# Cross-attention values in 32-column tiles of TensorE: the value blocks of two heads stationary, the probabilities moving, the softmax sums by selector matmuls

## What is computed

```python
q = (x @ Wq + bq).reshape(bs, n_ctx, HEADS, d)            # 16 batches x 256 tokens, 16 heads, d = 16
kv = (data @ Wkv + bkv).reshape(bs, n_data, HEADS, 2 * d) # 77 context rows
scores = jnp.einsum('bqhd,bkhd->bhqk', q, k) * scale
attn = jax.nn.softmax(scores, axis=-1)
out = jnp.einsum('bhqk,bkhd->bqhd', attn, v).reshape(bs, n_ctx, WIDTH)
return out @ Wp + bp
# then x = x + that; layer norms; router logits, top 2 of 8 experts, gates, gated expert FFN
```

## Time and profile before

| | us |
|---|---|
| median of 3 runs | 933.84 |
| lowest, highest | 932.91, 934.47 |
| the profiled execution | 936.83 |
| its span in the trace | 935.0 |
| attention rounds, about | 32 to 312 |

### The profile page before, as it was taken

One profiled execution on the slowest core, in us unless ns is written; L12 is line 12 of the kernel. 1 busy time (PEld: TensorE's weight loads), 2 busy tenths in 40 slices (PEclk: granted clock), 3 DMA queues, 4 the chain that ended last, 5 costly groups with the idle time before them and its releaser, 6 DMA issues.

```text
span 935.0 us, 19225 instructions
## 1 busy us (share of the span) xinstructions
PE 891.6 (95%) x6206; PEld 800.3 (86%) x6206; DVE 747.5 (80%) x1757; ACT 647.7 (69%) x1305; POOL 412.6 (44%) x649
## 2 busy tenths in 40 slices
PE   4999999999999999999999999999999999999994
PEld 3787888888878887888999999898898998998994
DVE  2677888888888889787979888887877877778883
ACT  3666767677676774776968777766876777677773
POOL 3455577777777667340432230505214234052042
PEclk9899999999999999999999999999999999999998
DMA  5332242343246337643755454826817737465442
GB/s 141 61 69 50 53 106 67 75 108 74 61 116 192 114 106 281 183 116 116 221 142 172 130 166 151 243 91 186 302 25 230 265 77 261 166 179 178 146 80 26
DMA packets 132626, 129.18 MB, mean 138 GB/s; under 512 B 59985, under 2 KB 117409, under 8 KB 132385
## 3 DMA queue, kind: packets, MB, share of 16 engines
q1 hardware_dynamic: 119648, 110.36, 38.2%
q0 software_dynamic: 12864, 17.44, 10.1%
HBM read 102.01 MB, written 25.36 MB: 136 GB/s over the span
## 4 chain that ended last, share of the span: by engine, by line
PE 79%; DVE 7%; ACT 5%; issue 4%; POOL 2%; SPq 1%; DMA 1%; ACTq 0%; DVEq 0%; POOLq 0%
PE bank L2002 35%; PE bank L2046 18%; PE bank L1835 7%; PE bank L1755 3%; PE bank L1994 3%; PE bank L1812 3%; PE bank L1773 2%; PE bank L2034 2%; PE bank L1971 1%; PE bank L1820 1%; DVE maxes L1256 1%; PE bank L1868 1%; PE bank L1858 1%; ACT q_t L943 1%; PE bank L1802 1%
## 5 line engine op out<-in xcount | busy, mean ns | idle before, releaser
L859 POOL DMA_INDIRECT out_rows<-yo,token x68 | 114.3, 1682 | 380.5 <-ACT yo L1111 314.7
L2002 PE MATMUL bank<-xh,wh 128*128 128x512 f32 (+1 forms) x672 | 234.2, 349 | 3.7 <-DVE gate_in L1628 3.1
L2002 PE MATMUL bank<-xl,wh 128*128 128x512 f32 (+1 forms) x672 | 228.4, 340 | 0.0
L2002 PE MATMUL bank<-xh,wl 128*128 128x512 f32 (+1 forms) x672 | 228.0, 339 | 0.0
L1604 DVE TENSOR_TENSOR wl<-raw,wh 128x1024 fp32r<-128x1024 f32 x126 | 152.4, 1220 | 12.9 <-ACT wh L1042 12.0
L2002 PEld LDWEIGHTS bank<-xh,wh 128*128 128x128 f32 x672 | 127.9, 190 | 17.9 <-DVE gate_in L1628 6.0
L2046 PE MATMUL bank<-wh,hh 128*128 128x256 f32 x496 | 142.1, 286 | 0.5 <-DVE yo L1663 0.3
L2046 PE MATMUL bank<-wh,hl 128*128 128x256 f32 x496 | 140.8, 284 | 0.0
L2046 PE MATMUL bank<-wl,hh 128*128 128x256 f32 x496 | 140.8, 284 | 0.0
L2002 PEld LDWEIGHTS bank<-xh,wl 128*128 128x128 f32 x672 | 127.5, 190 | 14.8
L2002 PEld LDWEIGHTS bank<-xl,wh 128*128 128x128 f32 x672 | 128.0, 190 | 10.7
(11 more groups left out here) (198 smaller groups left out, 1887.4 us busy)
## 6 DMA issues: line engine op xcount, KB each, us to landing
raw<-in_W SPq DMA_DIRECT2D x42, 1024.0 KB, 6.5
raw<-in_Wo SPq DMA_DIRECT2D x25, 1024.0 KB, 5.9
whole<-in_W SPq DMA_DIRECT2D x8, 1024.0 KB, 8.3
xs<-in_x SPq DMA_DIRECT2D x32, 128.0 KB, 2.6
out_rows<-x SPq DMA_DIRECT2D x32, 128.0 KB, 1.8
shared<-z_rows SPq DMA_DIRECT2D x7, 520.0 KB, 5.3
bo_row<-in_bo SPq DMA_DIRECT2D x25, 128.0 KB, 4.4
k_blocks<-k_parts SPq DMA_DIRECT2D x128, 19.2 KB
```

Source lines behind the costliest of these rows:

```text
L859: e.indirect_dma_start(out=out, out_offset=bass.IndirectOffsetOnAxis(ap=token[j % 4][:, s:s + 1], axis=0), in_=yo[j % 2][:, s, :], in_offs ...
L2002: mm = e.matmul(ps[:, h * cols:(h + 1) * cols], ws[split_before(j) % 2][:, w, c, m * P:(m + 1) * P], xx[j % 2][:, c, 0:cols], start=(h == ...
```

## The change

The values product is turned round. The probabilities' columns are now cut into five blocks for each half of eight heads (four of 128 keys, one of 104), ten in all as before, and `probs_t` is the moving operand, 128 tokens wide. The stationary operand is a piece of `v_blocks` of 32 columns, two heads. Its output goes to 32 of the 128 partitions (a quadrant `q`), so each matmul uses 32 columns of the array. Per half there are two passes `s` over the four quadrants, because the 154 keys of two heads lie in two neighbouring blocks: 16 matmuls. The result has the attention columns on the partitions and the tokens along the row, the form that `project` needs.

The column of ones is gone. `sum_probs` multiplies each block of `probs_t` with a constant 32-column selector, again in a quadrant (block number modulo 4), and leaves four partial sums per head. `sums_copy` on ScalarE takes values and sums out of PSUM together. One round later, right behind `scores(i, 0)`, `transpose_sums` adds the four quadrants and turns the sums with one matmul; VectorE takes the reciprocal (`invert_sums`), ScalarE repeats each one 16 times (`widen_inverses`), TensorE turns these (`spread_inverses`, the last step before `scores(i, 1)`) and VectorE multiplies (`normalize`, ahead of the second half of its softmax work), writing `attn_t`. `transpose_attn` and `attn_t_copy` are gone, and "spread" takes the place of "attn" among the bank turns, at another place. `sum_probs` waits for all three copies of the probabilities at once.

Around it: `load_values` issues four DMAs instead of two, `spread_values` four operations instead of six, a table `select` (128 x 336) is loaded at the start, VectorE clears the rows of `v_rep` that no load writes before `setup_ready`, and two small copies of `probs_t` become one.

```diff
@@ misc_turns
-        uses = [("attn", i - 2)] if 0 <= i - 2 < NT else []
-        uses += [("k", nb // 2)] if batch and even and nb % 2 == 0 else []
+        uses = [("k", nb // 2)] if batch and even and nb % 2 == 0 else []
         uses += [("v", nb)] if batch and even else []
         uses += [("q", nb)] if batch and not even else []
+        uses += [("spread", i - 2)] if 0 <= i - 2 < NT else []
         uses += [("logits", i - 5)] if 0 <= i - 5 < NT else []
@@ ScalarE
+            def sums_copy(i):
+                e.wait_ge(values_mm, i + 1)
+                if i:
+                    e.wait_ge(sums_t_mm, i)
+                    e.wait_ge(attn_made, i)
+                e.activation(sums[:, :], value_bank[:, 0:(DC + 1) * P], ACTF.Copy).then_inc(
+                    sums_out, 1)
+
+            def widen_inverses(i):
+                e.wait_ge(recip_made, i + 1)
+                if i:
+                    e.wait_ge(spread_mm, i)
+                e.activation(inverses[:, :].rearrange("p (h d) -> p h d", h=HEADS),
+                             recip[:, :].unsqueeze(2).broadcast_to([P, HEADS, HD]),
+                             ACTF.Copy).then_inc(inverses_out, 1)
...
-                    attn_t_copy(i - 2)
+                    widen_inverses(i - 2)
...
                     exp_scores(i, 1)
+                if before:
+                    sums_copy(i - 1)
@@ VectorE
+            def invert_sums(i):
+                e.wait_ge(sums_t_mm, i + 1)
+                if i:
+                    e.wait_ge(inverses_out, i)
+                at = (DC + 1) * P
+                e.reciprocal(recip[:, :], value_bank[:, at:at + HEADS]).then_inc(
                     recip_made, 1)
+            def normalize(i):
+                e.wait_ge(sums_out, i + 1)
+                e.wait_ge(spread_mm, i + 1)
+                if i >= 2:
+                    e.wait_ge(proj_mm, i - 1)
+                e.tensor_tensor(attn_t[i % 2][:, :, :].rearrange("p c k -> p (c k)"),
+                                sums[:, 0:DC * P], misc_of("spread", i)[:, 0:DC * P],
                                 ALU.mult).then_inc(attn_made, 1)
...
                     softmax_input(i, 0)
+                if 0 <= i - 2 < NT:
+                    invert_sums(i - 2)
...
+                if 0 <= i - 2 < NT:
+                    normalize(i - 2)
                 if 0 <= i < NT:
                     softmax_input(i, 1)
...
-                if 0 <= i - 1 < NT:
-                    normalized(i - 1)
@@ TensorE
+            def transpose_sums(i):
+                at = (DC + 1) * P
+                e.wait_ge(sums_out, i + 1)
+                if i:
+                    e.wait_ge(recip_made, i)
+                e.matmul(value_bank[:, at:at + HEADS], sums[:, DC * P:(DC + 1) * P], select[:, S_PICK:S_END],
+                         start=True, stop=True, skip_group_check=True).then_inc(sums_t_mm, 1)
+
+            def spread_inverses(i):
+                ps = claim("spread", i)
+                e.wait_ge(inverses_out, i + 1)
+                for m in range(DC):
+                    mm = e.transpose(ps[:, m * P:(m + 1) * P],
+                                     inverses[:, m * P:(m + 1) * P], ident)
+                mm.then_inc(spread_mm, 1)
...
+            def sum_probs(i):
...
+                e.wait_ge(probs_t_out, 3 * i + 3)
+                for k in range(KB):
+                    q, size = k % QUADS, P if k < KB - DC else TAIL
+                    mm = e.matmul(
+                        value_bank[q * QUAD:(q + 1) * QUAD, DC * P:(DC + 1) * P],
+                        select[0:size, S_SUM + k * QUAD:S_SUM + (k + 1) * QUAD],
+                        probs_t[i % 2][0:size, k, :], start=(k < QUADS),
+                        stop=(k + QUADS >= KB), skip_group_check=True)
+
             def values(i):
                 b = i // 2
-                if i:
-                    e.wait_ge(attn_made, i)
                 if i % 2 == 0:
-                    e.wait_ge(v_spread, 6 * (b + 1))
-                for k in range(KB):
-                    if k % 4 == 0:
-                        e.wait_ge(probs_t_out, 3 * i + k // 4 + 1)
-                    first, nh = block_heads(k)
-                    size = P if k < KB - 1 else TAIL
-                    mm = e.matmul(
-                        value_bank[:, first * VW:(first + nh) * VW], probs_t[i % 2][0:size, k, :],
-                        v_blocks[b % 2][0:size, k, 0:nh, :].rearrange("p j d -> p (j d)"),
-                        start=(k == 0), stop=(k == KB - 1), skip_group_check=True)
+                    e.wait_ge(v_spread, 4 * (b + 1))
+                for m in range(DC):
+                    for s in range(2):
+                        for q in range(QUADS):
+                            k, size = block_at(m, q + s), block_rows(q + s)
+                            mm = e.matmul(
+                                value_bank[q * QUAD:(q + 1) * QUAD, m * P:(m + 1) * P],
+                                v_blocks[b % 2][0:size, m, s, q, :, :].rearrange(
+                                    "p h d -> p (h d)"),
+                                probs_t[i % 2][0:size, k, :], start=(s == 0), stop=(s == 1),
+                                skip_group_check=True)
                 mm.then_inc(values_mm, 1)
...
                     scores(i, 0)
+                if 0 <= i - 2 < NT:
+                    transpose_sums(i - 2)
...
-                if 0 <= i - 2 < NT:
-                    transpose_attn(i - 2)
...
                     queries(nb)
+                if 0 <= i - 2 < NT:
+                    spread_inverses(i - 2)
...
                 if 0 <= i - 1 < NT:
+                    sum_probs(i - 1)
                     values(i - 1)
```

More of the change, by code:

```diff
@@ L34 @@
 KEYS = HEADS * CTX
-KB = -(-KEYS // P)
-TAIL = KEYS - (KB - 1) * P
-BLOCK_HEADS = 3
-VW = HD + 1
+HALF_KEYS = HPC * CTX
+JB = -(-HALF_KEYS // P)
+KB = DC * JB
+TAIL = HALF_KEYS - (JB - 1) * P
+QUAD = 32
+QH = QUAD // HD
+QUADS = P // QUAD
 WIDTH = 512
@@ L178, with block_at, block_rows, sum_selectors @@
 X_END = X_E + 1
-def block_heads(i):
-    first = i * P // CTX
-    last = min(i * P + P - 1, KEYS - 1) // CTX
-    return first, last - first + 1
+S_SUM = 0
+S_PICK = KB * QUAD
+S_END = S_PICK + HEADS
+def block_at(m, j):
+    return m * (JB - 1) + j if j < JB - 1 else DC * (JB - 1) + m
+def block_rows(j):
+    return P if j < JB - 1 else TAIL
+def sum_selectors():
+    c = np.zeros((P, S_END), np.float32)
+    p = np.arange(P)
+    for m in range(DC):
+        for j in range(JB):
+            at = S_SUM + block_at(m, j) * QUAD
+            key = j * P + p[0:block_rows(j)]
+            c[p[0:block_rows(j)], at + m * HPC + key // CTX] = 1.0
+    for q in range(QUADS):
+        c[q * QUAD + np.arange(HEADS), S_PICK + np.arange(HEADS)] = 1.0
+    return c
 def constants():
@@ L194, in constants @@
     c[:, C_IOTA:C_IOTA + P] = p[None, :]
-    for i in range(KB):
-        first, n = block_heads(i)
-        for j in range(BLOCK_HEADS):
-            c[:, C_VMASK + i * BLOCK_HEADS + j] = (i * P + p) // CTX == first + j
+    for s in range(2):
+        for q in range(QUADS):
+            for h in range(QH):
+                c[:, C_VMASK + (s * QUADS + q) * QH + h] = (
+                    ((q + s) * P + p) // CTX == q * QH + h)
     c[:, C_TOKEN:C_TOKEN + NT] = p[:, None] + P * np.arange(NT)[None, :]
@@ L382, in build @@
         q_l = [sb(f"q_l{i}", [P, DC, SEQ], F32R) for i in range(2)]
-        v_blocks = [sb(f"v_blocks{i}", [P, KB, BLOCK_HEADS, VW]) for i in range(2)]
+        v_blocks = [sb(f"v_blocks{i}", [P, DC, 2, QUADS, QH, HD]) for i in range(2)]
         probs = [sb(f"probs{i}", [P, HEADS, CTX]) for i in range(2)]
@@ L393, in build @@
         xs = [sb(f"xs{i}", [P, D]) for i in range(XR)]
-        attn = [sb(f"attn{i}", [P, D]) for i in range(2)]
+        select = sb("select", [P, S_END])
+        sums = sb("sums", [P, (DC + 1) * P])
         attn_t = [sb(f"attn_t{i}", [P, DC, P]) for i in range(2)]
-        recip = [sb(f"recip{i}", [P, HEADS]) for i in range(2)]
+        recip = sb("recip", [P, HEADS])
+        inverses = sb("inverses", [P, D])
         x1 = [sb(f"x1_{i}", [P, D]) for i in range(3)]
@@ L441, in build @@
         misc, (last_on_bank6, last_on_bank7) = misc_turns()
-        misc_read = {"ctx": lambda b: (ctx_t_out, b + 1), "attn": lambda i: (attn_t_out, i + 1),
+        misc_read = {"ctx": lambda b: (ctx_t_out, b + 1), "spread": lambda i: (attn_made, i + 1),
                      "q": lambda b: (q_out, 2 * b + 2), "proj": lambda i: (x1_made, i + 1),
@@ L816, in pool_program @@
             e.memset(zeros[:, :], 0.0).then_inc(zeros_ready, 1)
-            for i in range(2):
-                e.memset(v_sb[i][:, :, HD:VW], 1.0).then_inc(ones_ready, 1)
             e.memset(mv[:, :, :, :], 1.0).then_inc(mv_ready, 1)
@@ L1165, in drain_rest @@
                     logits_copy(i - 5)
+                if i - 1 < NT:
+                    sums_copy(i - 1)
+                if i - 5 < NT:
```

(11 more changed lines are left out.)

107 lines of the change are left out of this document (47 added, 60 removed).

## The result

The changed kernel takes 958.33 us (median of 4 runs, 955.48 to 961.61), beside it the kernel before 934.15 us (4 runs, 932.91 to 935.64). The ratio is 1.026, with a 95% interval of 1.022 to 1.030: slower by 24 us, where 43 were forecast. The profiled execution spans 956.4 us, against 935.0. So the sign was right and the sum was 19 us too high, and the trace shows that this was not one size a little off. The largest term had the wrong sign, and the loss lies where the sum put next to nothing.

The account below looks back on a forecast made before the run. The prediction took TensorE's queue as the bound. Its terms summed to +1.34 us a tile, times 32 = 43 us, plus 0.3, giving a forecast of 977 us; the range was 928 to 1005.

Parts of the forecast that it names:

- The values block: TensorE's selector and value matmuls: 52 instructions take 2.94 us against 2.15 before, +0.79 us a tile.
- four at a time: Rival for the values matmuls: all four quarters stream side by side, block 1.5 us, total time 931 us; chance 0.16.
- two-at-a-time case: Likeliest case for the values matmuls: two instructions stream together, block 2.94 us, total time 961 to 1003 us; chance 0.62.
- Change of tile shape: TensorE entering and leaving the 32-column tiles around the values matmuls: +0.1 us a tile (0 to 0.2).
- Turning the sums: `transpose_sums` on TensorE: +0.22 us a tile, plus 0.15 us of stall for ScalarE's `sums_copy`.
- Banks: New order of bank claims: `logits` inherits the wait on `q_t`, +0.4 us in odd rounds, +0.2 on average.
- Given back: TensorE's 5.1 us of waits for VectorE's subtraction: 4 us regained, -0.12 us a tile.
- Other engines: Value loads on SP's queue have 12 us of cover: no cost a tile, +0.3 us at the start.
- The high end: Upper end of the likeliest case's range: +2.15 us a tile, total time 1003 us.

Follow-up runs that it names:

- e1: The changed kernel with the 26 calls of the values block written quadrant by quadrant instead of round the quadrants: 1018.29 us.
- e4: The changed kernel with GpSimd's roots and bias sum ahead of `spread_values`, and the bank claims of `logits` (odd rounds) and `spread` (keys rounds) moved: 962.76 us, ratio 1.015.
- n1: The changed kernel with 16 selector matmuls repeating the sums in place, their way back removed, VectorE taking the 128 x 256 reciprocal: 972.19 us, 1.026 of the kernel before.
- n2: The changed kernel with sums repeated in place and their reciprocal made on ScalarE as exp(-ln(sum)), VectorE only multiplying: 974.61 us, 1.035 of the kernel before.
- e2: The changed kernel with GpSimd's roots and bias sum moved ahead of `spread_values`: 972.17 us, ratio 1.029 to the kernel before.

## Why the prediction was right in sign and wrong in its steps

- **The values block, +0.79 us.** This is the step that failed: "each call adds one step: 26 calls are 27 steps of 0.109". The step of 0.109 us was right. The order was not: instructions of a tile that is free pass those that wait, so it is fourteen steps (not thirteen, since the quarters have seven, seven, six and six calls), 1.45 us, plus 0.2 to the next tile shape. Measured -0.5 us from 2.15 to 1.66, the rival "four at a time" almost to the tenth (1.5 + 0.1). e1 shows the two-at-a-time case as another order of the same instructions. The chance given to this rival, 0.16, was too small: the scores' pair showed only what two tiles can do, and nothing in it bore on four.
- **Change of tile shape, +0.10.** The gap from the last start of the block to the next is 0.2 us, inside the 1.66. Right.
- **Turning the sums, +0.22 and a stall of 0.15.** `transpose_sums` takes 0.24 us (151.88 to 152.12). The stall does not show: L1846 has no wait in the list, and only the scores in front of it take 0.70 us instead of 0.62. Size right, stall some 0.1 too high.
- **Banks, +0.4 in odd rounds.** `logits` waits for `q_t` 0.6 us, 13 times, 7.6 us in all. From the last transposes to `project` odd rounds take 1.49 us (156.12 to 157.61), against 0.99 as the mean of before: +0.5. Right in this place, though odd rounds as a whole grew by 0.25 only. And the other half of the bank order was missed. In rounds with keys `spread` claims the keys' bank. I went through the claims of odd rounds only.
- **Given back, -0.12.** The wait for the subtraction is gone, all 5.1 us. "The chain recip, widen, spread then stands ahead of the same scores", the prediction says, and prices it at 1.1 us in all. The waits for `inverses` come to 8.4 us in the attention stretch and 5.6 behind it (0.97 and 4.59). This is the term that was too small.
- **Other engines, nothing.** The cover of `v_blocks` for its reader on TensorE was there, as said. What stood behind it on GpSimd's own queue was not asked: the roots, for `make_y`, for the keys' copy. 1.1 us in each round with keys, some 8 us.
- **The change-over to the experts.** It is no term of the sum, which multiplied by 32 as if the last tiles were like the others. 11 us.
- **The high end.** Its terms add up to +2.10 a tile and not to +2.15, so 1001 and not 1003. Nothing hangs on it.

The rival's sum is 931, and the time is 958. The 27 us between them lie in three places: the bank and GpSimd's order in rounds with keys and odd rounds (11 us by e4), the last tiles' inverses with the clock behind them (up to 11 us by the two timelines, with no experiment that gave them back), and the waits for `inverses` in the other rounds. That the forecast lay on the right side is luck. With the block as it measured (-0.49, its change of shape included) and every other term as it stands, the sum is 933 us: no change. The time came out slower through terms that were too small or missing. How the loss splits between the idle stretches and the lower clock is not shown, but has a bound: between 32 and 900 us the lower level covers 13.7 us in after and 6.8 in before, so it can account for at most some 7 of the 21 us (an estimate, half of 13.7).

No version tried beats the kernel before. The best of the changed form is e4, 1.5% above it. The way back of the sums can be taken off TensorE, as n1 and n2 show, but the reciprocal of sixteen times as many numbers then loads another engine so much that nothing is gained.

## What to carry to other kernels

Where a change puts small steps with an engine's turn between them into TensorE's queue, price each one's wait in every kind of round, and in the last ones, with what stands ahead of it on the other engine. Walk through the whole list of bank claims for each kind of round, since one claim more moves all behind it to the other bank. When an operand has its cover, ask also who stands behind the one that waits for it. And before two traces are compared round by round, set aside the rounds in which the granted clock was low: one such round turned the reading of e2, and one hid the gain in the even rounds.

## What the runs showed of the hardware

- Four tiles of 32 columns stream at once, one start per tile and 0.109 us, for float32 calls of two instructions each, if the order goes round the tiles. Instructions then start out of the program's order (159.12 ahead of 159.22). The block's last instruction, the one that signals its end, starts at 159.93, ahead of four others that start from 159.99 to 160.10. In a tile-by-tile order the same 52 take 3.05 us instead of 1.66.
- VectorE's reciprocal of 128 x 256 takes 1745 ns, four times its product of the same size (424 ns); for 128 x 16 it takes 0.25 us.
- A function table on ScalarE takes 1.28 us to load, and alternating exp and ln loaded one for each, 58 times in the attention stretch.
- The clock fell to its lower level in or within 2 us behind idle stretches of TensorE of 1 to 5 us in the change-over, and within 2 us behind waits of 1.7 to 1.8 us in attention rounds (once in after, at 279.9 us, and several times in n1, where the mean was 0.94). In before it fell once in these rounds, at 265.6 us, behind one of 0.77.
- The same kernel before took 934 to 948 us from group to group, and in three groups ScalarE and VectorE waited 1 to 2 us in many odd rounds of the variants, without a releaser in the profile. The cause is open.
